# Attention block on one core: a moved low part, the first image's T made two row tiles in turn, its scale and shift on GpSimd

## The chip, the cores and the metric

The kernel runs on one core of a Trainium2 chip. The metric is the device time of one execution in microseconds; the median of three runs is 2061.13 us (2060.94 to 2061.47). The core's engines are TensorE (PE; its weight loads are shown as PEld), VectorE (DVE), ScalarE (ACT), GpSimd (POOL) and SyncE (SP), which here only issues transfers. Each runs its own list of instructions in order and waits on semaphores for the others.

## The reference, cut to what matters

```
h    = group_norm(x, 32 groups) * gamma + beta        x: 16 images, 512 channels, 32 x 32
q, k, v = conv1x1(h, wq, bq), conv1x1(h, wk, bk), conv1x1(h, wv, bv)     N = 1024 places
attn = softmax(q^T k * 512**-0.5, over k's places)
out  = x + conv1x1(v attn^T, wo, bo)
```

All of it is in float32, from inputs of that type.

## The kernel before, in words

**Products in three terms.** TensorE multiplies float32 values as pairs: a high part (cast to a shorter form by ScalarE) and a low part (value minus high part, by VectorE). `product` (lines 380 to 383) is three matmuls: high by high, high by low, low by high. So each operand needs one cast and one subtraction before TensorE can take it, and that is most of what ScalarE and VectorE do. In the texts `high_x` is a cast and `low_x` a subtraction.

**The weights are folded.** In the head the kernel makes W_kq = wk by wq and W_ov = wo by wv once. An image is then five stages on TensorE: T = W_kq h (14 products of 6 matmuls of 512 columns), the scores h^T T (28 such products), V = h^T W_ov (28 products of 6 matmuls of 256 columns), outputs_0 and outputs_1, which are V times the exponentials P for the first and the second half of the places (each 4 x 8 groups of 3 matmuls). T, scores and V are made by a scheme with seven block products instead of eight; the sums that it needs are taken by VectorE: S1 to S4 of blocks of h (`sum_h`), D1, D2, D3, B11, B22, B21 of the products of T (`add_t`). Products gather in PSUM banks, so a bank's content must be copied out by ScalarE (`snap`, three snapshots a, b, y for each row tile) before the next product adds to it.

**T in detail.** T has two row tiles r. The products come in the order p = 4, 5, 2, 7, 6, 1, 3. Products 2, 6 and 3 wait for the snapshots a, b and y of their row tile, product 1 for the sum D3. In every image but the first, products 4, 7 and 5 wait for VectorE to have taken the outputs of the last image out of their banks (`o_scaled`). `make_t` (line 434) does all seven products for r = 0 and then all for r = 1.

**The loop.** TensorE's list for an image: make_t, make_scores, make_v, outputs_0, outputs_1. `outputs_1` (line 563) goes over four groups c of output rows, and in each over eight blocks n; in the first group, c = 0, it waits before block n for `p_split`, the low part `low_p(1, n)` of the second half's exponentials. VectorE's list for an image is in its `image` (from line 1168): T's sums and low parts, sums of the scores and maxima, `centre` (line 1075), the sums and low parts of V and `low_p` of the first half (1082), `centre` of the second half, `add_up` of the first half (1106 to 1110), `low_p` of the second half, and, if there is a next image, its `low_h` and `sum_h` (904, 889 to 897); then `add_up` of the second half, `inverse` (1117 to 1122), four `output` (1129), the other four `low_h`, `inverse`, four `output`. The order before the change stands in these lines:

```
for n in range(4, NJ - 1):
    low_p(b, 1, n)
if more:
    for n in range(3):
        low_h(b + 1, n)
    dve.wait_ge(sum_step, count(b, SUM_STEPS, 3))
    sum_h(b + 1, 0)
    sum_h(b + 1, 1)
low_p(b, 1, NJ - 1)
```

The last cast of P, for n = 7, waits on ScalarE for the end of outputs_0. ScalarE's list at an image's start: wait for all seven `low_h`; snapshot a; `bias_output(last)` (714) for outputs 4 and 5 of the last image, each of which waits for VectorE's `output`; snapshot b; `bias_output` 6 and 7; the cast of D3; snapshot y; the other casts. GpSimd issues the stores of outputs behind each `bias_output` (373); they add to what lies in `out`, where SyncE has copied x. VectorE's D3 of row tile 0 waits for the first four of these stores, D3 of row tile 1 for the last four, because the sums lie where the outputs lay.

**The first image.** Its statistics, scale and shift come in the head: VectorE takes mean and variance of groups, GpSimd rstd (336), VectorE `affine` (878 to 883: h_scale, mean_scaled, h_shift, 128 x 4 each), ScalarE normalises h in place (599). GpSimd takes the low parts of wv (331) that the products of W_ov wait for. ScalarE casts the seven weight blocks (615), VectorE takes their low parts (949, 953), then come `high_h`, `low_h` in the order H_FIRST. ScalarE also copies W_ov out of PSUM (`copy_wov`, 651). After T, VectorE's `first_weights` (1144 to 1149, 1141) makes four differences of W_ov and the low parts of seven blocks of it, and ScalarE casts these blocks (`high_wv`, 662): three before the scores, and one behind each of the first four snapshots of the scores. The fourth block is cast behind the first snapshot and waits for all four differences.

## Time and profile before

| | |
|---|---|
| median of 3 runs | 2061.13 us |
| the profiled execution | 2061.74 us |
| its span, first to last instruction | 2060.0 us |
| TensorE busy | 1991.7 us, 97% |
| TensorE weight loads busy | 1694.4 us, 82% |
| VectorE busy | 1636.6 us, 79% |
| ScalarE busy | 999.8 us, 49% |
| GpSimd busy | 329.3 us, 16% |
| mean granted clock of TensorE | 0.988 of 2.4 GHz |
| chain that ended last | PE 70%, DVE 10%, ACT 8%, issue 7% |

Matmuls are pipelined: each is shown with its duration (0.39 us for 512 columns at the full clock), but the next begins some 0.23 us later. So time between matmuls is read from their starts. Times are from the start of the span. The loop over images has the same pattern in each image, and the prediction takes one from the middle.

### The profile page before, as it was taken

To read this page: it belongs to the slowest core of one execution; us is meant where nothing else is said; L and a number is where in the kernel's file an instruction comes from. 1 tells how busy PE (TensorE), PEld (TensorE's weight loads), DVE (VectorE), ACT (ScalarE), POOL (GpSimd) and SP (SyncE) were. 2 spreads that over 40 slices of the span, in tenths; PEclk is the share of its full clock that TensorE was granted. 3 is DMA by queue.
4 is the path that set the end of the run, shared out by engine and by line. 5 is a ranking of instruction groups with operands and counts; after the bars stand their busy time and mean duration, and the time that the engine had idled before them with its cause. 6 is when DMAs were issued, how large, how long until landed. Compare 5 with 4: busy or idle time off the path is not lost.

```text
span 2060.0 us, 29828 instructions
## 1 busy us (share of the span) xinstructions
PE 1991.7 (97%) x9924; PEld 1694.4 (82%) x9924; DVE 1636.6 (79%) x2287; ACT 999.8 (49%) x1529; POOL 329.3 (16%) x238
## 2 busy tenths in 40 slices
PE   7999999999999999999999999999999999999998
PEld 6888878888787887878878788887888878788787
DVE  7897786978879688696887879778697886968856
ACT  6464453645436464454644536445364543646443
POOL 2012120111202022020121202212011120202202
PEclk9999999999999999999999999999999999999999
DMA  6435252362424534154351533525235242353302
GB/s 235 148 143 154 75 150 92 143 163 116 98 92 150 155 143 108 55 173 132 143 148 34 179 106 143 153 70 154 92 143 163 102 112 92 147 158 143 77 36 41
DMA packets 55467, 255.45 MB, mean 124 GB/s; under 512 B 8208, under 2 KB 8208, under 8 KB 50832
## 3 DMA queue, kind: packets, MB, share of 16 engines
q1 hardware_dynamic: 34896, 221.53, 28.1%
q0 software_dynamic: 18432, 33.56, 10.8%
q10 hardware_dynamic: 2112, 0.01, 0.1%
q8 instruction: 16, 0.26, 0.1%
q14 instruction: 11, 0.09, 0.0%
HBM read 214.18 MB, written 74.45 MB: 140 GB/s over the span
## 4 chain that ended last, share of the span: by engine, by line
PE 70%; DVE 10%; ACT 8%; issue 7%; DVEq 0%; ACTq 0%; POOL 0%; POOLq 0%
PE psum L381 24%; PE psum L382 23%; PE psum L383 23%; DVE h_lo L904 3%; ACT big_hi L708 2%; DVE big_lo L1082 2%; ACT room L599 2%; DVE big_lo L1098 2%; ACT scores L698 2%; ACT h_hi L608 2%; DVE scores L1075 1%; DVE scores L889 1%; DVE room L1089 1%; DVE red L1070 0%; DVE mean_scaled L880 0%
## 5 line engine op out<-in xcount | busy, mean ns | idle before, releaser
L381 PE MATMUL psum<-big_hi 128*128 128x512 f32 x1056 | 421.5, 399 | 53.6 <-DVE big_lo L1082 50.5
L382 PE MATMUL psum<-big_lo,big_hi 128*128 128x512 f32 x1056 | 419.2, 397 | 0.0
L383 PE MATMUL psum<-big_hi,big_lo 128*128 128x512 f32 x1056 | 418.9, 397 | 0.0
L381 PE MATMUL psum<-big_hi,h_hi 128*128 128x512 f32 x896 | 348.7, 389 | 0.0
L382 PE MATMUL psum<-big_lo,h_hi 128*128 128x512 f32 x896 | 348.6, 389 | 0.0
L383 PE MATMUL psum<-big_hi,h_lo 128*128 128x512 f32 x896 | 348.5, 389 | 0.0
L381 PEld LDWEIGHTS psum<-big_hi 128*128 128x128 f32 x1056 | 203.3, 192 | 102.7 <-DVE big_lo L1082 56.9
L1061 DVE TENSOR_TENSOR scores<-psum,room 128x512 f32<-128x512 f32 x192 | 130.7, 689 | 195.7 <-ACT room L764 145.7
L381 PE MATMUL psum<-w_split,h_hi 128*128 128x256 f32 x896 | 253.6, 283 | 0.1
L382 PE MATMUL psum<-w_split,h_hi 128*128 128x256 f32 x896 | 253.6, 283 | 0.0
L383 PE MATMUL psum<-w_split,h_lo 128*128 128x256 f32 x896 | 253.6, 283 | 0.0
L764 ACT COPY room<-psum 128x512 f32<-128x512 f32 x192 | 112.8, 587 | 288.2 <-PE psum L383 288.2
L383 PEld LDWEIGHTS psum<-big_hi,big_lo 128*128 128x128 f32 x1056 | 203.1, 192 | 43.5
L382 PEld LDWEIGHTS psum<-big_lo,big_hi 128*128 128x128 f32 x1056 | 203.4, 193 | 41.9
L1082 DVE TENSOR_TENSOR big_lo<-scores,big_hi 128x512 fp32r<-128x512 f32 x256 | 198.7, 813 | 24.9 <-ACT big_hi L708 24.9
L356 POOL PARTITION_ALL_REDUCE wide<-red x32 | 56.9, 1827 | 884.5 <-DVE red L1070 884.5
L381 PEld LDWEIGHTS psum<-big_hi,h_hi 128*128 128x128 f32 x896 | 168.2, 188 | 35.3 <-issue 0.5
L383 PEld LDWEIGHTS psum<-big_hi,h_lo 128*128 128x128 f32 x896 | 168.2, 188 | 34.9
L382 PEld LDWEIGHTS psum<-big_lo,h_hi 128*128 128x128 f32 x896 | 168.2, 188 | 34.8
L1075 DVE TENSOR_TENSOR scores<-scores,wide 128x1024 f32<-128x1024 f32 x128 | 162.9, 1324 | 32.7 <-POOL wide L356 32.7
L381 PE MATMUL psum<-h_hi,w_split 128*128 128x512 f32 x448 | 175.5, 392 | 5.9 <-DVE h_lo L904 5.9
L367 POOL PARTITION_ALL_REDUCE wide<-red x32 | 104.1, 3252 | 478.5 <-DVE red L1110 469.5
(126 smaller groups left out, 3453.9 us busy)
## 6 DMA issues: line engine op xcount, KB each, us to landing
w_split<-kept_t SPq DMA_DIRECT2D x15, 3584.0 KB, 11.8
w_split<-kept_v SPq DMA_DIRECT2D x15, 3584.0 KB, 11.3
room<-in_x SPq DMA_DIRECT2D x64, 512.0 KB, 3.4
out<-scores POOLq DMA_DIRECT2D x128, 256.0 KB, 6.1
room<-in_x SPq DMA_DIRECT2D x60, 256.0 KB, 5.5
red<-in_x SPq DMA_DIRECT2D x30, 256.0 KB, 3.1
wide<-in_x SPq DMA_DIRECT2D x30, 256.0 KB, 4.3
kept_t<-w_split SPq DMA_DIRECT2D x1, 3584.0 KB, 11.0
```

Source lines behind the costliest of these rows:

```text
L356: nc.gpsimd.partition_all_reduce(wide[:, half, :], red[:, half, :], P, MAX_ALL).then_inc(max_all, 1)
L367: nc.gpsimd.partition_all_reduce(wide[:, half, :], red[:, half, :], P, ADD_ALL).then_inc(sum_all, 1)
L381: nc.tensor.matmul(o, a_hi, b_hi, start=start, stop=False, skip_group_check=True)
L382: nc.tensor.matmul(o, a_hi, b_lo, start=False, stop=False, skip_group_check=True)
L383: return nc.tensor.matmul(o, a_lo, b_hi, start=False, stop=stop, skip_group_check=True)
L599: nc.scalar.activation(full[:, k, :], full[:, k, :], ACT.Identity, bias=h_shift[:, k:k + 1], scale=h_scale[:, k:k + 1]).then_inc(h_full, 1)
L608: nc.scalar.copy(h_hi[:, a, :, :], (first_blocks if first else blocks)[a]).then_inc(h_high, 1)
L764: nc.scalar.copy(snap_s(q, n), bank[alpha_s[q % 2]][:]).then_inc(s_snapped, 1)
L904: nc.vector.tensor_tensor(h_lo[:, a, :, :], (first_blocks if first else blocks)[a], h_hi[:, a, :, :].bitcast(F32), ALU.subtract).then_inc( ...
L1061: nc.vector.tensor_tensor(scores[:, o, :], bank[at][:], snap_s(q, n), ALU.add).then_inc(s_added, 1)
L1075: nc.vector.tensor_tensor(scores[:, j:j + 2, :], scores[:, j:j + 2, :], wide[:, half, :].unsqueeze(1).to_broadcast([P, 2, HALF]), ALU.subt ...
L1082: nc.vector.tensor_tensor(p_lo[:, j, :], scores[:, half * NJ + j, :], p_hi[:, j, :].bitcast(F32), ALU.subtract).then_inc(p_split, 1)
```

## The change

Three edits. VectorE takes `low_p(1, 7)` right behind `low_p(1, 6)` in every image, and the three `low_h` and four `sum_h` of the next image follow in one group. In the first image T's products are made for both row tiles in turn (p = 4 for r = 0, p = 4 for r = 1, p = 5 for r = 0, ...), by functions of their own on three engines (`make_first_t` on TensorE and on VectorE, `first_parts` on ScalarE); the snapshots and D3 of row tile 1 get places of their own, the semaphore counts alternate between row tiles, and the casts of h come in a new order. And the first image's scale and shift are made by GpSimd ahead of its low parts of wv; VectorE's `affine(0)` goes. The later images keep their functions, without the branches for the first.

```diff
+
+H_FIRST_HIGH = (A22, A12, S1, S3, A11, S2, S4)
+H_FIRST_HIGH_AT = {x: n + 1 for n, x in enumerate(H_FIRST_HIGH)}
...
+        snap_first = {"a": room[:, 1, :], "b": room[:, 3, :], "y": room[:, 5, :]}
+
+        def t_snap(first, r, name):
+            return snap_first[name] if first and r else scores[:, snap_t[name], :]
+
+        def t_sum(first, r, name):
+            return scores[:, 15 if first and r and name == "D3" else sum_t[r][name], :]
...
+        def t_count(b, first, per_row, r, step):
+
+            return 2 * (step - 1) + r + 1 if first else count(b, 2 * per_row, per_row * r + step)
...
             deviation(0)
+
+            pool.wait_ge(vec_in, 16 * len(vec_d))
+            pool.wait_ge(rstd_set, 1)
+            nc.gpsimd.tensor_tensor(h_scale[:], gamma_s, rstd[:], ALU.mult).then_inc(scale_step, 1)
+            pool.wait_ge(scale_step, 1)
+            nc.gpsimd.tensor_tensor(mean_scaled[:], chan_g_kv[:, :, 0], h_scale[:], ALU.mult).then_inc(scale_step, 1)
+            pool.wait_ge(scale_step, 2)
+            nc.gpsimd.tensor_tensor(h_shift[:], beta_s, mean_scaled[:], ALU.subtract).then_inc(scale_step, 1)
             for o in range(KC):
                 low_wv(o)
             prime()
...
+            def make_first_t():
+
+                pe.wait_ge(wt_split, 7)
+                for p in T_ORDER:
+                    pe.wait_ge(h_split, H_FIRST_AT[OF_H[p]])
+                    for r in range(2):
+                        if r == 1 and p == 5:
+
+                            pe.wait_ge(wov_copied, 2)
+
+                        if p in (2, 6, 3):
+                            pe.wait_ge(t_snapped, t_count(0, True, 3, r, {2: 1, 6: 2, 3: 3}[p]))
+                        if p == 1:
+                            pe.wait_ge(t_added, t_count(0, True, 6, r, C_AT["D3"]))
+                        t_product(0, r, p)
...
-                        pe.wait_ge(t_split, count(b, 14, 7 + L_AT[p]))
+                        pe.wait_ge(t_split, t_count(b, first, 7, 1, L_AT[p]))
...
-            for n in (1, 2, 3):
-                high_h(0, n, True)
...
+                elif r == 1:
+
+                    act.wait_ge(h_summed, 2)
+                    act.wait_ge(h_split, 1)
+                nc.scalar.copy(t_snap(first, r, name), bank[alpha_t[r]][:]).then_inc(t_snapped, 1)
...
+            def first_parts():
+                high_h(0, 2, True)
+                high_h(0, 1, True)
+                copy_wov(0)
+                copy_wov(1)
+                high_h(0, 3, True)
+                for r in range(2):
+                    snap(0, r, 0, "a", T_AT[4], True)
+                high_h(0, 5, True)
+                high_h(0, 4, True)
+                for r in range(2):
+                    snap(0, r, 1, "b", T_AT[2], True)
+                for r in range(2):
+                    high_t(0, r, "D3", True)
+                high_h(0, 6, True)
+                for r in range(2):
+                    snap(0, r, 2, "y", T_AT[6], True)
+                copy_wov(2)
+                copy_wov(3)
+                for name in G_ORDER[1:]:
+                    for r in range(2):
+                        high_t(0, r, name, True)
...
-                dve.wait_ge(h_high, count(b, 7, n + 1))
+                dve.wait_ge(h_high, H_FIRST_HIGH_AT[a] if first else count(b, 7, n + 1))
...
-            dve.wait_ge(vec_in, 16 * len(vec_d))
-            affine(0)
...
+            def make_first_t():
+
+                dve.wait_ge(wov_summed, KC)
+                add_t(0, 0, "D3", True)
+                low_h(0, 4, True)
+                low_h(0, 5, True)
+                sum_h(0, 3, True)
+                add_t(0, 1, "D3", True)
+                low_h(0, 6, True)
+                low_t(0, 0, "D3", True)
+                low_t(0, 1, "D3", True)
+                for name in C_ORDER[1:]:
+                    for r in range(2):
+                        add_t(0, r, name, True)
+                for name in L_ORDER[1:]:
+                    for r in range(2):
+                        low_t(0, r, name, True)
+
...
-                for n in range(4, NJ - 1):
+                for n in range(4, NJ):
                     low_p(b, 1, n)
                 if more:
                     for n in range(3):
                         low_h(b + 1, n)
 
                     dve.wait_ge(sum_step, count(b, SUM_STEPS, 3))
-                    sum_h(b + 1, 0)
-                    sum_h(b + 1, 1)
-                low_p(b, 1, NJ - 1)
-                if more:
-                    sum_h(b + 1, 2)
-                    sum_h(b + 1, 3)
+                    for n in range(4):
+                        sum_h(b + 1, n)
                 add_up(b, 1)
                 inverse(b, 0)
```

## Rows read from the trace of the kernel before

**Rows 1.** Waits of the whole span: engine, line, releaser: us in total, times, longest

```profile
DVE scores L974 <- DMA out<-scores: 14.3, 11, 3.2
...
PE psum L381 <- DVE big_lo L1082: 50.5, 15, 3.4
...
PE psum L381 <- DVE h_lo L904: 5.9, 4, 1.8
```

**Rows 2.** TensorE in order of time, one image: start, us, line, operands, count [idle before]

```profile
1177.09 0.39 PE L381 MATMUL psum<-h_hi,w_split 128*128 128x512 f32 x1
...
1280.69 0.39 PE L383 MATMUL psum<-big_hi,big_lo 128*128 128x512 f32 x1
...
1284.44 0.50 PE L381 MATMUL psum<-big_hi 128*128 128x512 f32 x1 [3.36 <-DVE big_lo L1082]
...
1303.20 0.39 PE L381 MATMUL psum<-h_hi,w_split 128*128 128x512 f32 x1
```

**Rows 3.** Windows behind that wait: length, engines' busy time, granted clock, DMA share

```profile
1286.00:1288.00 2.00, 2.00 (x6) 1.57 (x5) 2.00 (x2) 1.64 (x2) 0.00 (x0) 0.50 0.00 0
...
1290.00:1292.00 2.00, 2.00 (x10) 1.63 (x9) 1.90 (x5) 0.00 (x0) 0.83 (x1) 1.00 0.00 0
```

**Rows 4.** VectorE's sum D3 of row tile 0, images 1 and 15

```profile
172.79 0.75 DVE L974 SCALAR_TENSOR_TENSOR scores<-psum,t_step,scores 128x512 f32<-128x512 f32 x1 [2.05 <-PE psum L383]
...
1935.19 0.75 DVE L974 SCALAR_TENSOR_TENSOR scores<-psum,t_step,scores 128x512 f32<-128x512 f32 x1 [2.13 <-PE psum L383]
```

**Rows 5.** VectorE in order of time, the image of rows 2

```profile
1277.41 0.69 DVE L1082 TENSOR_TENSOR big_lo<-scores,big_hi 128x512 fp32r<-128x512 f32 x1 [0.78 <-ACT big_hi L708]
...
1278.02 3.49 DVE L904 TENSOR_TENSOR h_lo<-room,h_hi 128x1024 fp32r<-128x1024 f32 x3
...
1283.69 0.69 DVE L1082 TENSOR_TENSOR big_lo<-scores,big_hi 128x512 fp32r<-128x512 f32 x1
...
1292.76 2.48 DVE L1129 TENSOR_TENSOR scores<-psum,wide 128x512 f32<-128x512 f32 x4
...
1295.16 4.62 DVE L904 TENSOR_TENSOR h_lo<-scores,h_hi 128x1024 fp32r<-128x1024 f32 x4
...
1301.66 2.48 DVE L1129 TENSOR_TENSOR scores<-psum,wide 128x512 f32<-128x512 f32 x4
```

**Rows 6.** ScalarE in order of time, the same image

```profile
1276.77 1.13 ACT L708 CAST big_hi<-scores 128x512 fp32r<-128x512 f32 x2
...
1293.48 2.57 ACT L714 ACTIVATE scores<-scores,out_bias 128x512 f32<-128x512 f32 x4 [5.63 <-DVE scores L1129]
...
1304.76 0.59 ACT L669 COPY scores<-psum 128x512 f32<-128x512 f32 x1 [8.71 <-PE psum L383]
```

**Rows 7.** Stores of outputs 0 to 3, window 1294 to 1299: issues in ns, landing

```profile
L373 POOL DMA_DIRECT2D out<-scores x4: 1055/1363/1855, 1294.9 to 1296.7; - x4
DMA to landing us min/median/max: 3.9/6.2/8.3
```

**Rows 8.** TensorE in the first image

```profile
39.18 0.60 PE L381 MATMUL psum<-h_hi,w_split 128*128 128x512 f32 x1 [1.76 <-DVE h_lo L904]
...
71.81 0.39 PE L381 MATMUL psum<-big_hi,h_hi 128*128 128x512 f32 x1
```

**Rows 9.** VectorE in the first image, and an operation of a later one

```profile
22.59 0.83 DVE L878 TENSOR_TENSOR h_scale<-vecs,rstd 128x4 f32<-128x4 f32 x1
...
69.39 0.68 DVE L1149 TENSOR_TENSOR scores<-room,scores 128x512 f32<-128x512 f32 x1
...
1259.51 0.16 DVE L878 TENSOR_TENSOR h_scale<-vecs,rstd 128x4 f32<-128x4 f32 x1
```

**Rows 10.** ScalarE in the first image

```profile
25.96 2.38 ACT L599 ACTIVATE room<-room,h_shift,h_scale 128x1024 f32<-128x1024 f32 x2 [2.34 <-DVE h_shift L883]
```

**Rows 11.** GpSimd in the first image

```profile
20.36 1.06 POOL L336 TENSOR_TENSOR rstd<-var_g,minus_half 128x4 f32<-128x4 f32 x1 [2.53 <-DVE var_g L873]
...
22.14 5.03 POOL L331 TENSOR_TENSOR big_lo<-scores,big_hi 128x512 fp32r<-128x512 f32 x4 [0.71 <-ACT big_hi L633]
```

More of the change, by code:

```diff
@@ L572, in image @@
             def image(b, more, first=False):
-                make_t(b, first)
+                if first:
+                    make_first_t()
+                else:
+                    make_t(b)
                 make_scores(b, first)
@@ L715, in bias_output, with later_parts @@
                                      bias=out_bias[:, c:c + 1]).then_inc(o_done, 1)
-            def image(b, more, first=False):
-                if not first:
-                    act.wait_ge(h_split, count(b, 7, 7))
-                else:
-                    act.wait_ge(bias_summed, 1)
+            def first_parts():
[20 more added lines that the diff above has]
+                        high_t(0, r, name, True)
+            def later_parts(b):
+                act.wait_ge(h_split, count(b, 7, 7))
                 for r in range(2):
@@ L725, in image @@
                         snap(b, r, 0, "a", T_AT[4])
-                        if first:
-                            copy_wov(0)
-                            copy_wov(1)
-                        else:
-                            for n in (KC, KC + 1):
-                                bias_output(b, n, last=True)
+                        for n in (KC, KC + 1):
+                            bias_output(b, n, last=True)
                     snap(b, r, 1, "b", T_AT[2])
-                    if r == 0 and first:
-                        high_h(0, 4, True)
-                        high_h(0, 5, True)
-                    elif r == 0:
+                    if r == 0:
                         for n in (KC + 2, KC + 3):
@@ L740, in image @@
                     snap(b, r, 2, "y", T_AT[6])
-                    if r == 0 and first:
-                        high_h(0, 6, True)
                     high_t(b, r, "D1")
@@ L750, in image @@
                     high_t(b, r, "B21")
-                    if r == 0 and first:
-                        copy_wov(2)
-                        copy_wov(3)
+            def image(b, more, first=False):
+                if first:
+                    act.wait_ge(bias_summed, 1)
+                    first_parts()
+                else:
+                    later_parts(b)
                 if first:
@@ L967, in _, with add_t, made @@
             sum_h(0, 2, True)
-            def add_t(b, r, name):
-                o = scores[:, sum_t[r][name], :]
+            def add_t(b, r, name, first=False):
+                o = t_sum(first, r, name)
+                def made(other):
+                    dve.wait_ge(t_added, t_count(b, first, 6, r, C_AT[other]))
+                    return t_sum(first, r, other)
                 if name == "D3":
-                    dve.wait_ge(t_summed, count(b, 14, 7 * r + T_AT[5]))
-                    dve.wait_ge(t_snapped, count(b, 6, 3 * r + 1))
+                    dve.wait_ge(t_summed, t_count(b, first, 7, r, T_AT[5]))
+                    dve.wait_ge(t_snapped, t_count(b, first, 3, r, 1))
@@ L1022, in make_t @@
+            def make_t(b):
+                for n in range(KC):
+                    dve.wait_ge(out_stored[n], count(b, 16, 0))
+                add_t(b, 0, "D3")
+                low_t(b, 0, "D3")
                 add_t(b, 0, "D1")
@@ L1028, in make_t @@
                 low_t(b, 0, "B11")
-                if not first:
-                    for n in range(KC, 2 * KC):
-                        dve.wait_ge(out_stored[n], count(b, 16, 0))
+                for n in range(KC, 2 * KC):
+                    dve.wait_ge(out_stored[n], count(b, 16, 0))
                 add_t(b, 1, "D3")
@@ L1168, in image @@
             def image(b, more, first=False):
-                make_t(b, first)
                 if first:
+                    make_first_t()
                     first_weights()
+                else:
+                    make_t(b)
                 step = 0
```

106 lines of the change are left out of this document (39 added, 67 removed).

## The prediction

> **What bounds the kernel now.** I read the busy shares of the table first: TensorE is busy for nearly the whole span, VectorE for 79%. So I then read the list of waits for what TensorE still waits for, and only that. One pair stands out: line 381 waits for VectorE's line 1082 15 times, 50.5 us in all, 3.4 at the longest [rows 1]. 15 is the number of images that have a next one. TensorE's instructions in order show the wait in an image of the middle: the matmul of 1280.69 should be followed 0.227 us later, at 1280.92, and is followed at 1284.44 [rows 2]. The reader should look on: from 1286 to 1288 the granted clock is 0.50 (1.2 GHz), six matmuls are under way in 2 us, and from 1290 it is 1.00 (2.4 GHz) with ten [rows 3]. Nothing else of that size slows the loop: from the first product of one image's T (1177.09) to 1280.92 are 103.83 us, and the 75 matmuls left (3 for c = 0, 24 for each other c) take 17.0 at 0.227. An image without the wait is 120.83 us. The first T sums of image 1 and of image 15 lie 1762.40 us apart, 125.89 an image [rows 4]. So this one wait, with the slow clock behind it, costs 5.06 us an image, 75.9 us over 15.
>
> What is late there is the last low part of the second half of P, low_p(1, 7). VectorE makes it at 1283.69, after 5.7 us of work for the next image: three low_h (3.49 us from 1278.02) and two sums [rows 5]. ScalarE's cast for it is the second of a pair that ends at 1277.90 [rows 6].
>
> **Part 1: the order of low parts in VectorE's image().** After the edit low_p(1, 7) follows low_p(1, 6), which begins at 1277.41. The next operation can begin at 1278.02, the cast is there at 1277.90, so the part is done at 1278.71; TensorE wants it at 1280.92, 2.2 us later [rows 2, 5, 6]. The wait goes, and there is no gap for the clock to fall behind. The three low_h and two sums slip by 0.6 us; nothing reads them before the next image but ScalarE's casts, which have no other work then. VectorE's work behind them begins when it did, since the sum of its queue is the same. Term A: minus 75.9 us.
>
> What is late next? TensorE reaches the next T at 1280.92 + 17.0 = 1297.93 instead of 1303.20 [rows 2]. VectorE doesn't: from 1278 its queue is full until the four outputs of 1301.66 end at 1304.14. I go through T (a product is 6 matmuls, 1.36 us).
> - Third product (p = 2, due 1300.65): needs the first snapshot. ScalarE waits for all low_h, done at 1299.78 [rows 5], and copies for 0.59 us [rows 6]: in time.
> - Fifth product (p = 6, due 1303.37): needs the second snapshot. In ScalarE's order two bias_output(last) stand ahead of it, and they wait for VectorE's outputs of 1301.66 and, 0.6 later, 1302.26. The group of the first half shows the lag: outputs from 1292.76, biases from 1293.48, four of them 0.62 apart [rows 5, 6]. So biases at 1302.38 and 1303.00, the snapshot from 1303.61 to 1304.20. TensorE stands 0.9 us, and about 0.1 more for the first matmul behind a wait: 1.0.
> - Sixth product (p = 1, then due 1305.7): needs the sum D3, which waits for the first four stores of the last image. They are issued from 1294.9 to 1296.7 and land 3.9 to 8.3 us later [rows 7]; the last, I take it, at 1305.0. VectorE is free at 1304.1, so D3 runs from 1305.0 to 1305.75. That can be late by 0 to 0.7 us; I take 0.3, nearer to the shown image.
> - Second row tile: its D3 waits for the last four stores, for which VectorE stood 11 times before, 3.2 us at the longest [rows 1]. Their biases move up with the snapshots, by 3.9 us, and TensorE by 5.27 - 1.3 = 3.97: as before, so nothing.
> VectorE then ends T's low parts as far behind TensorE as before, and has its idle 21% in the scores to get level.
> Term B, a new wait of 1.3 us an image. Bounds: 0 (stores and snapshot early) and 3.05 (1.7 us of standing, and a fallen clock as after the old one, which cost 5.06 - 3.36 = 1.7, less what the shorter gap spares). 15 times 1.3 = plus 19.5 us.
>
> Here a rule of the Trainium skill can be weighed. The row says 3.9 to 8.3 us from issue to landing for stores of 256 KB that add to their target [rows 7]. The page "DMA: Bandwidth & Descriptors", in "Anatomy of one DMA — SWDGE (gpsimd) path", fits such a transfer as about 2.0 us plus its bytes over 436 GB/s, an estimate of 2.6 us here. By that rule D3 never waits and term B would be 1.0 an image, 15 us. This trace does not agree, and the sum goes by the row.
>
> **Part 2: both row tiles in turn, first image.** T is 14 products of 6 matmuls, 19.0 us in any order. In the order of before four of them wait for low_h, 5.9 us in all, and after one of 1.76 us the matmuls of 39 to 43 us take 0.60 instead of 0.39 [rows 1, 8]. With two products per block, a block has 2.7 us to arrive. I followed the three queues through the new order with the durations shown. VectorE's three scale operations leave (22.59 to 25.85, 3.3 us) [rows 9]. ScalarE normalises from 23.6, where its casts end, instead of 25.96 [rows 10]; the weight parts and low_h 0 come 2.6 us earlier. Behind that VectorE waits some 1.9 us less, so T's low parts end at 63.0 instead of 67.4. TensorE, from 34.7 on without a wait, is through T at 53.8, 8.5 us early. It can't keep that. ScalarE's fourth cast of the V weights stands in its queue ahead of the second snapshot of the scores, and waits for the fourth subtraction of first_weights, done at 70.07 before [rows 9] and now at 65.65. Cast and snapshot end at 66.85, and the product p = 6, q = 1, due at 63.3, stands 3.6 us. Before it ran at 71.81 [rows 8]. That is a gain of 4.9, less up to 1.7 if the clock falls behind this gap as it does behind 3.4 us. Term C: minus 4; bounds minus 1 (below) and minus 6.5 (VectorE's queue 1.6 us quicker). The other snapshot places, the counts and the buffers change no instruction's shape and cost nothing.
>
> **Part 3: scale and shift by GpSimd.** No row has this operation there. The nearest are the power on the same 128x4, 1.06 us, and the subtractions of 512 columns, 5.03 for four, 1.26 each [rows 11], of which 4 columns are next to nothing. An operation costs between 0 and 1.06; I take 0.25, nearer to the plain subtraction's start-up than to a power. Three end at about 22.3, beside the start of the first low_wv (22.14) that TensorE waits for. At 1.06 each they end at 24.8: the products of W_ov start 2.6 us later, and ScalarE normalises 1.1 us earlier instead of 2.3. TensorE's delay then falls into its 3.6 us of standing, ScalarE's takes 2 us off term C, and with a fallen clock minus 1 is left.
> VectorE took 0.83 us for the first of these in this stretch and 3.3 for the three with what lies between, but 0.16 for one in a later image [rows 9]; in the stretch GpSimd runs its four low_wv [rows 11]. "GPSIMD Engine Reference", section 3.1 (Elementwise — side-by-side cycle accounting), gives VectorE some 156 ns of dispatch and GpSimd two software hops, which speaks against the move: by it the three are worth 0.5 us on VectorE, part 3 gains nothing, and term C is about minus 2. The later image agrees with it, the first image doesn't.
>
> **Sum.** The profiled execution took 2061.7 us (its span of 2060.0 and 1.7 around it), 0.6 over the median of the runs, 2061.1. 2061.7 - 75.9 + 19.5 - 4 = 2001.3; I say 2001.
>
> **Rivals.**
> - No new wait: stores land early and the snapshot is hidden. 2061.7 - 75.9 - 4 = 1982. Against it, the fifth product rests on fixed rows.
> - The clock falls at the new waits. They are 1.0 and 0.3 to 0.7 us, with 1.36 of work between. 3.05 instead of 1.3: 15 times (5.06 - 3.05) = 30, with 3 of the first image 2028. For it: one wait of 1.76 us, shortly behind another, was followed by slow matmuls [rows 8]. Against it: four waits of up to 1.8 us came there, and only one fall.
> - Not faster. low_p(1, 7) now stands ahead of VectorE's work for the next image, and its cast waits for the end of outputs_0. If VectorE is held there, add_up, the outputs of 1301.66 and the snapshot slip one for one. To eat 5.06 us it must be held by 3.8 us on top of the 1.3; at 4.2 the time is 2064. Outputs_0 ends 4.8 us before 1280.92, at 1276.2; the cast begins at 1277.3 and ends 0.1 before VectorE comes [rows 2, 5, 6]. I see nothing that moves these by 4.
> - The first image gains nothing (dear GpSimd operations, the clock fallen twice): 2005.
>
> **How the numbers follow.** Forecast 0.62, no new wait 0.12, clock falls 0.15, first image gains nothing 0.07, not faster 0.04. The likeliest one's own range is 1993 to 2012. The range of 1984 to 2028 leaves out most of the case without a wait and the one of not faster. Less than 0.2%, 4 us, could not be told from no change. Faster 0.96, same 0.02, slower 0.02.
>
> **What would show it.** Line 1082 gone from TensorE's waits; in its place about 1 us for ScalarE's snapshot and a few tenths for D3 in each of 15 images; an image of 122.1 us; VectorE waiting for the stores before D3 of the first row tile; the scores of image 0 begun near 54 us, with one wait of 3 to 4 us near 63. Wrong: a clock of 0.50 still in every image, a wait of another kind above 2 us, or an image of 121 or of 124 us.

## The result, and the profile after

| | before | after |
|---|---|---|
| median | 2061.03 us | 2031.36 us |
| lowest and highest of four runs | 2059.91, 2061.47 | 2030.86, 2034.50 |
| span of the profiled execution | 2060.0 us | 2029.9 us |
| VectorE busy | 1636.6 us | 1630.4 us |

The ratio is 0.986 (95%: 0.9843 to 0.9877). The change gains 30 us; I had forecast 60, with a range that ended at 2028. So the direction was right and half of the gain is missing.

The page of the kernel after begins as follows (span; busy time by engine; the chain that ended last, by engine).

```profile
span 2029.9 us, 29828 instructions
PE 1985.6 (98%) x9924; PEld 1678.9 (83%) x9924; DVE 1630.4 (80%) x2284; ACT 999.5 (49%) x1529; POOL 325.8 (16%) x241
PE 81%; DVE 7%; DMA 7%; issue 3%; ACT 2%; POOL 0%; DVEq 0%; SPq 0%; POOLq 0%; ACTq 0%
```

The new entry in the chain is a DMA with 7%. Which one, the list of waits says (engine and line, releaser: us in total, times, longest).

```profile
DVE scores L1028 <- DMA out<-scores: 63.7, 23, 5.4
...
PEld psum L406 <- DVE scores L1028: 29.0, 21, 2.5
...
PE psum L406 <- DVE scores L1028: 20.3, 17, 2.1
```

```profile
PE psum L406 <- ACT scores L704: 8.9, 15, 0.8
```

The line numbers have moved: 406 to 408 are a product's matmuls (381 to 383 before), 1139 is low_p, 1028 the sum D3 (974 before), 704 the snapshot, 749 the bias, 398 the stores. The wait for low_p of [rows 1], 50.5 us in 15 places, has no line of this kind any more. But VectorE now stands 63.7 us for the stores instead of 14.3, and TensorE stands for VectorE's D3.

TensorE's rows of one image, the image whose T began at 1303.20 in [rows 2]:

```profile
1279.38 0.39 PE L406 MATMUL psum<-h_hi,w_split 128*128 128x512 f32 x1
...
1285.71 0.50 PE L406 MATMUL psum<-h_hi,w_split 128*128 128x512 f32 x1 [0.59 <-ACT scores L704]
...
1298.04 0.50 PE L406 MATMUL psum<-h_hi,w_split 128*128 128x512 f32 x1 [1.12 <-DVE scores L1028]
```

The first begins the image's T. The second is the product p = 6 of row tile 0, behind the second snapshot. The third is the product p = 1 of row tile 1, behind its D3: the wait that I had counted at nothing. VectorE's rows of the two D3 of this image, and of row tile 1's D3 in the last image:

```profile
1286.30 0.75 DVE L1028 SCALAR_TENSOR_TENSOR scores<-psum,t_step,scores 128x512 f32<-128x512 f32 x1 [0.69 <-DMA out<-scores]
...
1297.23 0.75 DVE L1028 SCALAR_TENSOR_TENSOR scores<-psum,t_step,scores 128x512 f32<-128x512 f32 x1 [4.42 <-DMA out<-scores]
...
1916.21 0.75 DVE L1028 SCALAR_TENSOR_TENSOR scores<-psum,t_step,scores 128x512 f32<-128x512 f32 x1 [1.58 <-PE psum L408]
```

VectorE stands 4.42 us before D3 of row tile 1, for stores. In the last image, where no input of a next image is loaded, this D3 waits for its matmul and for no store. Windows at and behind the waits (length, TensorE, weight loads, VectorE, ScalarE, GpSimd, granted clock, DMA share, GB/s):

```profile
1286.00:1288.00 2.00, 2.00 (x10) 1.53 (x10) 1.01 (x2) 1.81 (x4) 2.00 (x4) 1.00 0.75 108
1295.00:1297.00 2.00, 1.92 (x9) 1.26 (x7) 0.00 (x0) 0.00 (x0) 0.00 (x0) 1.00 0.80 157
...
1299.00:1301.00 2.00, 2.00 (x9) 1.34 (x8) 2.00 (x5) 0.12 (x1) 0.00 (x0) 1.00 0.00 0
```

The clock stays at 1.00 behind both waits of this image. It does so in 14 of the 15 images with such waits. The exception is image 12, where TensorE stood longest, 2.08 us, and the clock fell; its T is 24.02 us long, the longest of all (TensorE's row, and the window behind it):

```profile
1546.90 0.61 PE L406 MATMUL psum<-h_hi,w_split 128*128 128x512 f32 x1 [2.08 <-DVE scores L1028]
```

```profile
1547.00:1549.00 2.00, 2.00 (x5) 1.53 (x6) 2.00 (x4) 0.98 (x2) 0.00 (x0) 0.53 0.00 0
```

Back to the image shown. Between 1295 and 1297 VectorE, ScalarE and GpSimd all stand still, and the DMA engines are busy for 0.80 of the time: this is what VectorE waits for. The rows that tell why are the issues, GpSimd's and SyncE's, from 1285.2 on.

```profile
1285.20 3.52 POOL L398 DMA_DIRECT2D out<-scores  x4 [5.13 <-ACT scores L749]
```

```profile
1285.77 0.85 SPq L291 DMA_DIRECT2D red<-in_x  x2
...
1286.80 0.88 SPq L291 DMA_DIRECT2D wide<-in_x  x2
```

And the DMA view of the last four stores, after and then before: issues (ns, first and last start), then the time from issue to landing.

```profile
L398 POOL DMA_DIRECT2D out<-scores x4: 853/1004/1194, 1285.2 to 1287.5; - x4
DMA to landing us min/median/max: 4.7/8.1/9.4
```

```profile
L373 POOL DMA_DIRECT2D out<-scores x4: 853/972/1137, 1306.7 to 1309.9; - x4
DMA to landing us min/median/max: 4.7/5.2/5.6
```

In the kernel before, ScalarE's biases stood in two pairs behind snapshots that waited for TensorE, so the stores came in pairs, issued 2.4 and 5.0 us behind the first load. ScalarE's rows of before show the pairs (the first snapshot is the one of 1304.76 in [rows 6]), GpSimd's the stores, SyncE's the load:

```profile
1305.24 1.34 ACT L714 ACTIVATE scores<-scores,out_bias 128x512 f32<-128x512 f32 x2
1307.48 0.59 ACT L669 COPY scores<-psum 128x512 f32<-128x512 f32 x1 [0.90 <-PE psum L383]
1307.96 1.34 ACT L714 ACTIVATE scores<-scores,out_bias 128x512 f32<-128x512 f32 x2
```

```profile
1306.69 1.74 POOL L373 DMA_DIRECT2D out<-scores  x2 [8.09 <-ACT scores L714]
1309.32 1.75 POOL L373 DMA_DIRECT2D out<-scores  x2 [0.89 <-ACT scores L714]
```

```profile
1304.31 0.85 SPq L274 DMA_DIRECT2D red<-in_x  x2
```

Now TensorE is ahead of VectorE, the biases follow the outputs at once, and so do the loads: four stores and four loads are issued within 3 us. The last store lands after 9.4 us instead of 5.6. The image shown is a kind one for the kernel before: over the 14 images with loads, the last store takes 5.6 to 8.5 us there (median 6.5) and 9.4 to 10.3 (median 9.9) in the kernel after. In the last image, without loads, it takes 6.8 in the kernel after. SyncE's loads of its wide tiles, 30 of them, pay as well: 4.3 us to landing in the page of before, 8.3 in this one.

```profile
wide<-in_x SPq DMA_DIRECT2D x30, 256.0 KB, 8.3
```

**An account by stage.** Stage lengths are differences of TensorE's starts, in us. O is the stage of both outputs, outputs_0 and outputs_1. Means of images 1 to 14:

| | before | after | difference an image |
|---|---|---|---|
| O, with the wait for low_p | 48.6 | 43.55 | -5.0 |
| T | 19.07 | 22.3 | +3.2 |
| scores | 38.09 | 38.21 | +0.1 |
| V | 20.15 | 20.15 | 0 |
| image | 125.88 | 124.19 | -1.69 |

Fourteen of these images give -23.6. Image 1 begins at 162.32 instead of 169.77: -7.45, of which 5.3 are the wait for low_p in image 0's O and 2.1 the first image's own. The last image has a T of 20.38, +1.3, and what follows TensorE's last matmul is 0.3 shorter. Together -30.1, which is 2029.9 - 2060.0, the difference of the spans.

The pattern of before was not quite the same in each image. The wait for low_p is 3.36 to 3.40 us in all 15, but behind it the clock fell in 13 alone. In images 3 and 14 it stayed, and their O is 47.2 us instead of 48.6 to 48.9. So the slow clock behind the wait cost 1.6 us where it came.

### The profile page after: what moved, and what is told of

It reads as the page before. It is cut to its first block, busy times and chain, and to the rows that moved or that the text cites. A ratio compares the mean times of both kernels' runs of the same rounds, so it can differ in the third digit from the quotient of the medians.

```text
span 2029.9 us, 29828 instructions
## 1 busy us (share of the span) xinstructions
PE 1985.6 (98%) x9924; PEld 1678.9 (83%) x9924; DVE 1630.4 (80%) x2284; ACT 999.5 (49%) x1529; POOL 325.8 (16%) x241
## 4 chain that ended last, share of the span: by engine, by line
PE 81%; DVE 7%; DMA 7%; issue 3%; ACT 2%; POOL 0%; DVEq 0%; SPq 0%; POOLq 0%; ACTq 0%
PE psum L406 27%; PE psum L407 27%; PE psum L408 27%; DMA out<-scores 6%; DVE h_lo L955 3%; DVE scores L1186 1%; ACT scores L749 1%; DVE scores L1028 1%; DVE wide L1179 0%; DVE red L1174 0%; ACT scores L704 0%; DVE big_lo L1053 0%; DMA scores<-in_wq 0%; DVE bn L886 0%; DVE big_lo L1139 0%
## 5 line engine op out<-in xcount | busy, mean ns | idle before, releaser
L406 PE MATMUL psum<-big_hi 128*128 128x512 f32 x1056 | 411.9, 390 | 2.8 <-POOL big_lo L348 2.8
L407 PE MATMUL psum<-big_lo,big_hi 128*128 128x512 f32 x1056 | 411.9, 390 | 0.0
L408 PE MATMUL psum<-big_hi,big_lo 128*128 128x512 f32 x1056 | 411.5, 390 | 0.0
L406 PEld LDWEIGHTS psum<-big_hi 128*128 128x128 f32 x1056 | 198.8, 188 | 44.3 <-DVE big_lo L980 3.0
L408 PEld LDWEIGHTS psum<-big_hi,big_lo 128*128 128x128 f32 x1056 | 198.7, 188 | 41.4
L407 PEld LDWEIGHTS psum<-big_lo,big_hi 128*128 128x128 f32 x1056 | 198.7, 188 | 40.8
L406 PE MATMUL psum<-h_hi,w_split 128*128 128x512 f32 x448 | 180.8, 404 | 29.4 <-DVE scores L1028 20.3
L407 PEld LDWEIGHTS psum<-big_lo,h_hi 128*128 128x128 f32 x896 | 168.6, 188 | 34.7
```

The source lines that it names most:

```text
L406: nc.tensor.matmul(o, a_hi, b_hi, start=start, stop=False, skip_group_check=True)
L407: nc.tensor.matmul(o, a_hi, b_lo, start=False, stop=False, skip_group_check=True)
L408: return nc.tensor.matmul(o, a_lo, b_hi, start=False, stop=stop, skip_group_check=True)
```

## The experiments

Two theories stood after the comparison. **Collision**: the biases, and so the stores, and SyncE's four loads for the next image are now released by the same event (outputs taken), share the DMA engines, and the stores land late. **Chain**: the lateness is ScalarE's and VectorE's queue (outputs, biases, snapshot, sums), and the stores only end it. A side question was whether the wait for the stores is needed at all, and another what each small part is worth. Each ratio below is against the kernel before, run beside it. The first four were run in one comparison (2061.04 us for the kernel before), the last four in another (2061.28), so of differences between the two groups 0.2 us are the groups' own.

**order_only.** The kernel before with the order of the low parts alone.

```
-                for n in range(4, NJ - 1):
+                for n in range(4, NJ):
                     low_p(b, 1, n)
                 if more:
-                    sum_h(b + 1, 0)
-                    sum_h(b + 1, 1)
-                low_p(b, 1, NJ - 1)
-                if more:
-                    sum_h(b + 1, 2)
-                    sum_h(b + 1, 3)
+                    for n in range(4):
+                        sum_h(b + 1, n)
```

> The kernel before with part 1 alone: low_p(1, 7) ahead of the next image's low_h and sum_h; first image and scale as before. Theory: all of the gain and all of the new waits of the changed kernel but 2 us come from this edit. Then 15 outputs stages of 43.6 us instead of 48.7, T stages of 22 us instead of 19.0, and 2033.5 us in all (2031.4 plus the 2.1 us by which image 1 begins earlier in the changed kernel beyond its outputs stage). Rival: the new first image disturbs the later ones (its buffers or the phase at which image 1 starts), then T stages near 20.5 here and a time below 2015.

Measured: 2030.93 us (2029.25 to 2031.57), ratio 0.9851 (0.9834 to 0.9867). The whole gain of the change is in this edit. O is 43.55 and T 22.2 on the mean here too, and the list of waits has the same new line:

```profile
DVE scores L974 <- DMA out<-scores: 60.5, 25, 5.7
...
PE psum L381 <- DVE scores L974: 18.3, 18, 2.3
```

I had expected 2033.5 us here, because in the comparison of before and after the new first image had seemed to give 2.1 us. That does not show, and term C below says why.

**x_pieces_late.** The kernel after; SyncE issues four of the next image's six loads only after the ninth product of T, when the stores have landed.

```
-                    sp.wait_ge(o_scaled, count(b, 8, 8))
+                    sp.wait_ge(t_summed, count(b, 14, 9))
                     for n in range(2, 6):
                         piece(n)
```

> The changed kernel with the loads of pieces 2 to 5 of the next image's x held back until the fifth... the ninth product of T (p = 5 of row tile 1) is done, some 10 us later than now. Theory, collision: the last four output stores land 8 to 9 us after issue instead of 5 to 6 because the x pieces are issued within the same 3 us; without them they land in 5 to 6.5, D3 of row tile 1 runs when its product is done, the wait of TensorE before p = 1 of row tile 1 (1.1 to 2.0 us) and the 0.33 at the start of the scores go: 14 images by 2.0, 2003 us. Rival, queueing: the stores are slow because four follow each other without a gap; then they land as late as now and the time is 2031 us.

Measured: 2004.92 us (2003.57 to 2005.65), ratio 0.9727 (0.9711 to 0.9743). Nothing was changed for ScalarE, VectorE or GpSimd; only four loads come later. The last four stores of the same image:

```profile
L398 POOL DMA_DIRECT2D out<-scores x4: 853/1002/1191, 1267.6 to 1269.9; - x4
DMA to landing us min/median/max: 4.0/6.0/6.8
```

```profile
1276.64 0.85 SPq L291 DMA_DIRECT2D red<-in_x  x2
```

The loads come 6.7 us behind the last store's issue, and the last store lands after 6.8 us instead of 9.4 (6.3 to 7.2 over the 14 images, where the kernel after has 9.4 to 10.3). VectorE's stand for stores falls by two thirds:

```profile
DVE scores L1028 <- DMA out<-scores: 22.6, 23, 2.0
```

So the collision is the cause of the late landing, and four stores in a row, the rival, are not: they still follow each other without a gap here. The issues of GpSimd take as long as in the kernel after (1002 ns against 1004), and the wide tiles' loads are back at 4.1 us. T is 20.4 on the mean and the scores are 38.08.

**stores_by_slot.** The kernel after; in place of all four stores ahead of each D3, VectorE waits for a store only before the operation that writes over its source. D3 and D1 of row tile 1 overwrite none.

```
-                for n in range(KC):
-                    dve.wait_ge(out_stored[n], count(b, 16, 0))
+                stored(0)
                 add_t(b, 0, "D3")
                 low_t(b, 0, "D3")
+                stored(1)
                 add_t(b, 0, "D1")
+                stored(2)
                 add_t(b, 0, "D2")
+                stored(3)
                 add_t(b, 0, "B11")
...
-                for n in range(KC, 2 * KC):
-                    dve.wait_ge(out_stored[n], count(b, 16, 0))
                 add_t(b, 1, "D3")
...
                 add_t(b, 1, "D1")
+                stored(4)
                 add_t(b, 1, "D2")
+                stored(5)
                 add_t(b, 1, "B11")
+                stored(6)
                 add_t(b, 1, "B22")
+                stored(7)
                 add_t(b, 1, "B21")
```

> The changed kernel with VectorE's waits for the output stores put at the sum that really overwrites a store's source: D3, D1, D2, B11 of row tile 0 wait for stores 0 to 3 one by one, D2, B11, B22, B21 of row tile 1 for stores 4 to 7; D3 and D1 of row tile 1, whose places no store reads, wait for none. Theory: the new loss in T is these waits; the 1.1 to 2.0 us before p = 1 of row tile 1, the 0.33 at the scores and the 0.1 to 0.5 before p = 1 of row tile 0 go, ScalarE's snapshot (0.88) stays: T of 20.1 us, 15 times (3.1 - 1.0) less, 2000 us. Rival: the late landing only moves to D2 and B21 of row tile 1, whose low parts TensorE needs in the scores: then waits of 1 us or more in the scores and 2010 to 2025 us.

Measured: 1999.04 us (1998.80 to 2000.09), ratio 0.9700 (0.9683 to 0.9716). Loads and stores still collide, but nobody waits for the end of it. No line of VectorE for stores is left in the list; TensorE's part for the snapshot is:

```profile
PE psum L406 <- ACT scores L704: 9.1, 15, 0.8
```

T is 20.08 in images 2 to 14, so the snapshot's wait, with the 0.1 of p = 2, is 1.0 us an image; scores are back at 38.08, so the 0.13 there were a trace of the same lateness; an image is 121.87. The rival, that the wait only moves on to the scores, is out.

**snapshot_first.** The kernel after; ScalarE takes the second snapshot ahead of the two biases.

```
                         snap(b, r, 0, "a", T_AT[4])
-                        for n in (KC, KC + 1):
-                            bias_output(b, n, last=True)
                     snap(b, r, 1, "b", T_AT[2])
                     if r == 0:
-                        for n in (KC + 2, KC + 3):
+                        for n in range(KC, 2 * KC):
                             bias_output(b, n, last=True)
```

> The changed kernel with ScalarE's snapshot b of row tile 0 ahead of the biases of outputs 4 and 5. Theory, one chain: the snapshot's wait (0.88 us) goes, but TensorE then comes 0.9 us earlier to p = 1 of row tile 1, which waits for stores that are issued no earlier, so its wait grows by as much or, since the stores are issued 0.5 us later, by 1.4: 2030 to 2038 us. Rival, the waits add up: 15 times 0.88 less, 2018 us.

Measured: 2034.39 us (2031.32 to 2038.22), ratio 0.9873 (0.9857 to 0.9890). The wait for the snapshot is gone from the list, and nothing is won: TensorE comes 0.9 us earlier to D3's product and stands there. It does so at row tile 0's D3, not at row tile 1's as expected: the delay at p = 1 of row tile 0 grows from 0.3 to 1.0 us on the mean, that of row tile 1 stays at 1.5.

```profile
DVE scores L1026 <- DMA out<-scores: 59.4, 21, 5.4
...
PE psum L406 <- DVE scores L1026: 31.8, 28, 2.1
```

28 waits of 31.8 us, where the kernel after has 17 of 20.3. The two waits are one behind the other on one chain, and waits for stores end it.

**slots_snapshot.** Both edits, of stores_by_slot and snapshot_first.

```
                         snap(b, r, 0, "a", T_AT[4])
-                        for n in (KC, KC + 1):
-                            bias_output(b, n, last=True)
                     snap(b, r, 1, "b", T_AT[2])
                     if r == 0:
-                        for n in (KC + 2, KC + 3):
+                        for n in range(KC, 2 * KC):
                             bias_output(b, n, last=True)
...
-                for n in range(KC):
-                    dve.wait_ge(out_stored[n], count(b, 16, 0))
+                stored(0)
                 add_t(b, 0, "D3")
...
```

> stores_by_slot (1999.0 us) and snapshot_first together: VectorE waits for each output store where its source is overwritten, and ScalarE takes snapshot b of row tile 0 ahead of the biases of outputs 4 and 5. Theory, one chain: with the stores off the path the snapshot's 0.88 us is a gain now, though it was none alone: T of 19.2 us in images 1 to 15, 15 times 0.9 less, 1985.5 us. Rival: TensorE comes still earlier and D3 of row tile 0 (its store 0, or ScalarE's later cast of D3) becomes the next wait and takes it back: T near 20 us and 1995 to 2000 us.

Measured: 1989.22 us (1989.14 to 1990.55), ratio 0.9652 (0.9638 to 0.9667). The same edit that gave nothing gives 9.8 us by the medians once the stores are off the path. It was to give 13.5: T comes to 19.52, not 19.2, for three short waits stay, of 0.1 to 0.2 us each. An image is 121.30. By the traces T gives 15 times 0.56, 8.4 us. The other 1.5 us between the two profiled executions lie ahead of the first T (it begins at 35.02 here, at 36.54 in stores_by_slot), where the kernels are the same. ScalarE's biases, moved behind the snapshot, do not get shorter by standing together: four take 2.56 us, about what two pairs of 1.34 took.

**slots_old_first.** stores_by_slot without the first image's new order and without GpSimd's scale and shift (order of the low parts and waits by slot on the kernel before, against which the edit is shown).

```
             def make_t(b, first):
+                def stored(n):
+                    if not first:
+                        dve.wait_ge(out_stored[n], count(b, 16, 0))
...
-                    for n in range(KC):
-                        dve.wait_ge(out_stored[n], count(b, 16, 0))
+                    stored(0)
                     add_t(b, 0, "D3")
...
-                for n in range(4, NJ - 1):
+                for n in range(4, NJ):
                     low_p(b, 1, n)
```

> stores_by_slot without parts 2 and 3: the kernel before, with the low parts in the new order and a wait for each output store where its source is overwritten; first image and scale as before. With the stores off the path the two differ in the first image alone. Theory: parts 2 and 3 give 1 to 2 us, because the 5.5 us that T gets shorter (19.0 instead of 24.5) come back in the scores (43.2 instead of 38.1), and the rest is V's wait and the head: 2000.5 us against 1999.0. Rival: they give the 4 us of the forecast: 2003 us.

Measured: 2000.09 us (1999.92 to 2000.12), ratio 0.9703 (0.9690 to 0.9716). Against stores_by_slot that is 1.05 us for both parts together. The first T is 24.53 us here, 19.04 there; the scores behind it 38.08 here, 43.20 there. What T gains, the scores give back all but 0.4 us.

**slots_scale_vector.** stores_by_slot with scale and shift made by VectorE, as before.

```
-            nc.gpsimd.tensor_tensor(h_scale[:], gamma_s, rstd[:], ALU.mult).then_inc(scale_step, 1)
...
-            nc.gpsimd.tensor_tensor(h_shift[:], beta_s, mean_scaled[:], ALU.subtract).then_inc(scale_step, 1)
...
+            affine(0)
```

> stores_by_slot with the first image's scale and shift made by VectorE again, as before the change (part 3 undone, part 2 kept). Theory: VectorE needs 3.3 us for the three small operations beside GpSimd's low parts of wv, where GpSimd needs 0.8 for them; ScalarE normalises 2.3 us later and T's low parts end 2.6 later, so TensorE's wait in the scores of image 0 grows by that: 2001.3 us against 1999.0. Rival: by VectorE's dispatch alone (0.16 an operation, as in later images) it is worth less than 0.5 us: 1999.0.

Measured: 2001.26 us (2000.19 to 2001.74), ratio 0.9707 (0.9694 to 0.9720): 2.2 us above stores_by_slot. That difference, and the 1.05 of slots_old_first, are small against the intervals of the ratios, some 3 us to either side, and by themselves show nothing. The traces separate the parts better, from the start of the first T to the start of image 1, which leaves out a head that differs by up to 1.5 us between executions: 125.94 us in stores_by_slot, 126.30 without both parts, 128.03 without part 3 alone. So part 3 is worth 2.1 us, the new order of the first T by itself costs 1.7, and both together give 0.4, in one execution of each. VectorE's row of the first of the three operations in this run (the other two take 1.20 each), and GpSimd's of the same operation in the kernel after:

```profile
22.38 0.92 DVE L922 TENSOR_TENSOR h_scale<-vecs,rstd 128x4 f32<-128x4 f32 x1
```

```profile
21.53 0.20 POOL L368 TENSOR_TENSOR h_scale<-vecs,rstd 128x4 f32<-128x4 f32 x1
```

**all_three.** slots_snapshot, and in the first image ScalarE's last four casts of the V weights two snapshots later.

```
                             nc.scalar.copy(snap_s(q, n), bank[alpha_s[q % 2]][:]).then_inc(s_snapped, 1)
-                            if first and pair == 0 and n < 2:
-                                high_wv(3 + 2 * n + q)
+                            if first and pair == 0 and n:
+                                high_wv(3 + 2 * (n - 1) + q)
```

> slots_snapshot and, in the first image, ScalarE's last four casts of the V weights each two snapshots later (behind the snapshots of products 6 and 5 and not of 1 and 6). Theory: in the first image's scores TensorE's wait of 3.2 us for the snapshot behind that cast, with the slow clock after it, costs 5.1 us (the scores take 43.2 instead of 38.1); of that 3.5 to 4.4 come back, since a wait of 0.7 is left at product 5, q = 1, and the snapshot of product 1, q = 2, waits for VectorE's sum C11: 1981.5 us. Rival: VectorE's own lateness (T's low parts end at 64.5 us) only shows at another product of the scores, and the first image keeps its length: 1985.5 us.

Measured: 1987.41 us (1986.79 to 1989.26), ratio 0.9643 (0.9629 to 0.9656), the fastest by the median (slots_snapshot: 1989.22). I had expected 1981.5, with 3.5 to 4.4 us from the first image. It gave 1.1: from the start of the first T to the start of image 1 are 124.82 us, where slots_snapshot has 125.95. The two spans are both 1987.6, since the head of this execution is 0.9 us longer. The scores are 40.80 instead of 43.20, for the wait of 3.21 and the slow clock behind it are gone, but another snapshot stands for VectorE's sum, and V takes 21.43 instead of 20.15. So the rival expectation, that VectorE's own lateness shows at another product, is nearer. ScalarE's rows of the cast and of that snapshot:

```profile
66.74 0.62 ACT L693 CAST w_split<-scores 128x512 fp32r<-128x512 f32 x1 [1.43 <-DVE scores L1211]
...
81.39 1.18 ACT L813 COPY room<-psum 128x512 f32<-128x512 f32 x2 [8.49 <-DVE scores L1123]
```

## Why the prediction was right or wrong

**Term A, the old wait: right.** -75.9 forecast; O fell from 48.6 to 43.55 on the mean, 5.04 us in 15 images, -75.6. The low part is made right behind the one before it, no gap is left there for the clock to fall behind, and order_only shows that no other part of the change has to do with it. VectorE's order in the kernel after is the one foreseen:

```profile
1258.88 1.29 DVE L1139 TENSOR_TENSOR big_lo<-scores,big_hi 128x512 fp32r<-128x512 f32 x2 [0.78 <-ACT big_hi L743]
1260.09 3.49 DVE L955 TENSOR_TENSOR h_lo<-room,h_hi 128x1024 fp32r<-128x1024 f32 x3
```

**Third, fifth and sixth product: right.** Nothing but 0.1 us at p = 2. The fifth product was to be 1.0 late, and T of stores_by_slot, where nothing else is late, is 1.04 longer than before. ScalarE's rows show the reason as given, two biases ahead of it:

```profile
1283.85 1.34 ACT L749 ACTIVATE scores<-scores,out_bias 128x512 f32<-128x512 f32 x2 [1.81 <-DVE scores L1186]
1285.09 0.56 ACT L704 COPY scores<-psum 128x512 f32<-128x512 f32 x1
```

D3 of row tile 0 was to cost 0.3 and costs 0 to 0.7, about 0.25 on the mean.

**Second row tile: the step that failed.** I wrote that its D3 waits for the last four stores, that their biases move up by 3.9 us and TensorE by 3.97, "as before, so nothing". The shift of the issue was right: counted from the start of O, the last of these stores goes out 3.9 us earlier than before. Counted from the start of the image's T it goes out 8.1 us behind (1287.5 against 1279.38) and not 6.7 (1309.9 against 1303.20 [rows 2]). Of the 1.4 more TensorE's own new waits ahead of that D3 take 1.0 in this image. What failed is the time to landing, which I took over silently from the order of before, without asking what else comes to the DMA engines then. SyncE's loads follow the outputs in both kernels; the stores did not follow them at once before and do now. The last takes 9.4 us instead of 5.6. In the kernel before, row tile 1's D3 began only 0.3 us behind the landing of that store (1309.9 + 5.6), as it waited for its matmul until then. So nearly all of the 3.8 us is lateness of D3, and what TensorE had in hand does not cover it. VectorE's row of before:

```profile
1315.79 0.75 DVE L974 SCALAR_TENSOR_TENSOR scores<-psum,t_step,scores 128x512 f32<-128x512 f32 x1 [0.27 <-PE psum L383]
```

The delay at p = 1 of row tile 1 is 0.9 to 3.4 us an image, 1.75 on the mean (the 3.4 is image 12, its slow clock included), and 0.3 to 0.4 follow at the first scores products. Term B is 3.4 an image in images 1 to 14 (against an unwaited T of 19.04: 3.25 in T, 0.13 in the scores) and 1.3 in the last: some 48.6 us for 19.5 forecast. The difference, 29 us, is nearly the whole error; the first image gave 2 us less than forecast on top. My upper bound for term B was 3.05, made of a fallen clock, so it could not hold this. The forecast of 1.3 is met where there are no loads: T of the last image is 1.3 longer. With the loads late, so that the stores land in time for that D3, the kernel takes 2004.9, and without waits for stores 1999.0. That the forecast of 2001 lies between the two is no merit; it is what the kernel takes if the failed step were true.

Of the signs that I had listed, "VectorE waiting for the stores before D3 of the first row tile" came (0.69 us in the image shown). So did two of the signs of being wrong: an image of 124 us (124.19), and "a wait of another kind above 2 us" (VectorE's 4.42, for the stores).

**Term C, the first image: mechanism right, size off.** T is 19.04 us without a wait, as forecast, and the scores begin at 55.42 (54 forecast; T itself began at 36.38, not 34.7). Then the product p = 6, q = 1 stands behind ScalarE's cast for VectorE's subtraction, as forecast:

```profile
66.44 0.68 DVE L1206 TENSOR_TENSOR scores<-room,scores 128x512 f32<-128x512 f32 x1
```

```profile
67.16 0.62 ACT L693 CAST w_split<-scores 128x512 fp32r<-128x512 f32 x1 [4.15 <-DVE scores L1206]
```

```profile
68.31 0.50 PE L406 MATMUL psum<-big_hi,h_hi 128*128 128x512 f32 x1 [3.21 <-ACT room L815]
```

```profile
70.00:72.00 2.00, 2.00 (x6) 1.57 (x5) 1.14 (x3) 1.10 (x2) 0.00 (x0) 0.50 0.00 0
```

The wait is 3.21, where I had 3.6, but the clock of 0.50 behind it brings the loss to 5.1 us (43.20 - 38.08). The product runs at 68.31 instead of 71.81, 3.5 us earlier where I had 4.9, and the slow clock takes some 1.7 of that. I had this fall in the bounds and not in the 4.

That is against the one execution that I counted from, and it was a slow one in this place. The first T took 26.50 us in the profiled execution of before, with a fall of the clock from 39.4 to 42.8 us. order_only and slots_old_first have the same first image, and there it took 24.50 and 24.53, without a fall in T. They had one at the head instead, from 24 to 28 us, as the kernel after has, and the profiled execution of before has none there (windows of before, order_only and after):

```profile
25.00:28.00 3.00, 3.00 (x15) 2.46 (x14) 2.93 (x5) 2.04 (x2) 2.17 (x2) 1.00 0.02 5
25.00:28.00 3.00, 3.00 (x9) 2.32 (x8) 2.96 (x4) 1.75 (x2) 2.43 (x2) 0.50 0.02 5
25.00:28.00 3.00, 3.00 (x8) 2.33 (x8) 1.56 (x3) 3.00 (x6) 2.35 (x2) 0.50 0.02 5
```

So the fall at the head is not made by the change: it comes with the old head too, and slots_snapshot, with the new head, has none. In the profiled executions image 1 begins 2.1 us earlier by this part, but only 1.0 earlier than in order_only, and the pair stores_by_slot and slots_old_first gives 0.4. Forecast 4, bounds 1 and 6.5.

**Part 3: right in kind.** GpSimd takes 0.20 for an operation (0.25 taken), 0.92 to 1.20 on VectorE in this stretch. It is worth 2.1 us by the traces, and here "GPSIMD Engine Reference", section 3.1 (Elementwise — side-by-side cycle accounting), of the Trainium skill does not help: its 156 ns of dispatch on VectorE hold in the later images, 0.16 us [rows 9], and not beside GpSimd's low_wv.

**The rivals.** "The clock falls at the new waits" gave 2028, near the measured 2031.4, and is wrong as the cause: the clock fell in one image of 15, which cost some 1.2 us in all. "No new wait" is wrong too. The estimate of 2.6 us for a store of 256 KB, from "DMA: Bandwidth & Descriptors" of the Trainium skill, section "Anatomy of one DMA — SWDGE (gpsimd) path", would have put term B at 15 us. The trace disagrees: the last four stores took 4.7 to 9.4 us in the image shown, and with no load beside them, in x_pieces_late, still 4.0 to 6.8.

## What to carry to other kernels

When a wait of TensorE is removed, write down for the transfers behind it both ends: the event that issues each queue's transfers, and the one that waits for their landing; a transfer time read in the old order holds only as long as no other queue's transfers are released by the same event. Then ask what each wait for a store protects: here D3 of the second row tile waited for four stores and overwrote the source of none, and moving the waits to the overwriting operations gave as much again (32 us) as the change itself (30). And of two waits on one chain the earlier is worth nothing until the later is gone, so try them together before giving one up.

## What the runs showed of the hardware

- The time from issue to landing of an accumulating store of 256 KB depends on what is issued beside it. For the last of four, over 14 images: 5.6 to 8.5 us (median 6.5) in two pairs behind the loads, 6.3 to 7.2 (6.6) for four in a row with none of these loads near (x_pieces_late), 9.4 to 10.3 (9.9) with four loads of 256 KB issued in the same 3 us. The loads pay too, 8.3 instead of 4.3 for the wide tiles.
- TensorE's granted clock did not follow the length of a wait alone. Behind waits of 3.36 to 3.40 us in the kernel before it fell to 0.50 (1.2 GHz) in 13 of 15 images. In the T stages of the kernel after, order_only and snapshot_first it fell behind waits of 2.07 to 2.30 us, four of them, and not behind any up to 1.95. In the first image of before it fell behind one of 1.76, with another wait of 1.07 shortly ahead of it.
- At the head, TensorE stands for the same 2.79 us in three kernels, and from 25 to 28 us the clock was 1.00 in the kernel before and 0.50 in order_only, which has the same head, and in the kernel after (rows of before, then after). So two executions of the same instructions can differ here, and a fall of the clock seen in one trace is not a cost of every execution.

```profile
23.56 0.47 PE L381 MATMUL psum<-big_hi 128*128 128x512 f32 x1 [2.79 <-POOL big_lo L331]
```

```profile
23.76 0.47 PE L406 MATMUL psum<-big_hi 128*128 128x512 f32 x1 [2.79 <-POOL big_lo L348]
```

- VectorE's operations on 128x4 take 0.16 us in a later image and 0.83 to 1.22 us beside GpSimd's low_wv; GpSimd's own take 0.20. VectorE's operations on 128x512 take 0.68 us beside low_wv, no more than elsewhere. No run takes low_wv away, so that it is the cause is not shown.
